# A decoder layer on one core: where the causal mask of the row-maximum pass is added

## The chip, the cores and the metric

The kernel runs on one core of a Trainium2 chip. The metric is device time in microseconds (us): 653.34 us is the median of three runs of the kernel before, which lie between 652.88 and 656.06.

## The reference

A decoder layer with post-norm: causal self-attention, cross-attention to 64 context rows, a mixture of 16 experts of which each token takes 4, and a shared expert, each followed by a layer norm. x is 2 x 1024 x 256 in float32; 16 heads of 16. The change touches the first part alone:

```python
scores = jnp.einsum('bhqd,bhkd->bhqk', Q, K) / math.sqrt(d_k)
causal = jnp.tril(jnp.ones((seq_len, seq_len), dtype=bool))
scores = jnp.where(causal, scores, -jnp.inf)
probs = jax.nn.softmax(scores, axis=-1)
attn = jnp.einsum('bhqk,bhkv->bhqv', probs, V)
```

## The kernel before

**Projection phase** (list `P1`, the first 76 us). Eight tiles of Q or K (`QK`, n = 0 to 7), each 128 x 1024, are projected by TensorE (L1526). So that bf16 products reach float32 accuracy, each tile is cut into three bf16 parts: ScalarE takes the first (L772), VectorE the rest (L978), ScalarE the second (L777), GpSimd the third (L670). SP stores the three parts to DRAM (`qk_parts`, L517). There are two buffers, so ScalarE's tile n waits for the store of tile n - 2 (L770). V is projected in eight further steps (`v`, L1541), the last four behind the last Q/K tile.

**Stacks.** The 32 heads (2 batches x 16) are handled in 8 groups of 4. For a group, `load_stack` (L486) brings 6 combinations of parts of Q and of K from DRAM into `qs` and `ks`, 12 transfers of 128 KB; they fill contraction rows 0 to 95 (`KR`). Three sets of stacks rotate (`g % 3`). Set 0 is loaded behind tile 1's store, set 1 behind tile 4's, set 2 behind the first row maxima, the others behind the B products of the group that used the set. In rows 96 to 98 (`KR` to `KM`) K has ones and Q the negative row maximum in three bf16 parts. The ones are written once, by GpSimd's first instruction, for rows 96 to 127 of all three sets (L657); rows 99 to 127 are never read. VectorE's first instruction waits for that memset and for all the others at GpSimd's start (`filled`, L934).

**A pass (row maxima).** 38 jobs a group (`A_JOBS`): TensorE multiplies a tile of 128 queries with up to 512 keys over 96 rows (L1471), VectorE takes the maximum (L947). Three PSUM banks rotate, so job n waits until VectorE is through with job n - 3 (L1468). Where the last 128 columns lie on the diagonal, a second product per head adds the mask: the identity matrix times `causA`, which has -1e30 above the diagonal (L1476). That is 32 products a group.

**Chain of the maxima ("M").** VectorE joins the maxima and cuts them into three bf16 parts, TensorE transposes them (L1496), ScalarE copies them to `mrow` (L800), SP spreads them with three transfers into rows 96 to 98 of `qs` (L531). The next group's B pass waits for all three (`m_loaded`, L1484).

**B pass.** 24 jobs a group: transposed scores minus the maximum over 99 rows (L1488), exponential on ScalarE (L791), the diagonal's upper part set to zero on GpSimd (L690), the product with V (L1512). `step_order` (L99) writes one order for all engines: each group's B jobs with the A jobs of the next group between them (30 in slots 0 to 16), M at slot 19, and the first 8 A jobs of the group after the next in slots 17 to 23. Before group 0's B jobs come 8 A jobs of group 1.

The queue of SP is in program order: loads, stores, stacks, the three transfers of M, and the row sums. A DMA raises its semaphore by 16 when it has landed.

Of the kernel before, what the change touches and what calls it, by code (L numbers as in the profile page):

```python
# [31 lines left out]
P = 128  # L32
# [17 lines left out]
NEG = -1e30  # L50
MASKED = -4e15
HG = 4
# [7 lines left out]
KM = KR + 3  # L60
CH = 512
# [127 lines left out]
def build(nc, a, out, qk_parts, l_dram, slots, sums_of, marks):  # L189
    with ExitStack() as ctx:  # L190
# [97 lines left out]
        causA = sb("caus_a", [P, P], BF16)  # L288
# [48 lines left out]
        earlier = causA  # L337
# [131 lines left out]
        def _(sp):  # L469
# [13 lines left out]
            for dst, name in ((identb, "identb"), (causA, "causA")):  # L483
                sp.dma_start(dst[:], a[name]).then_inc(ld_caus, 16)

            def load_stack(g, which=(0, 1)):  # L486
                b, o, g2 = g // GB, g % GB // 2, g % 2
                for t in which:
                    dst, split = ((qs, SPLIT_Q), (ks, SPLIT_K))[t]
                    for at, part in enumerate(split):  # L490
                        src = qk_parts[t, b, o, part, 64 * g2:64 * g2 + 64, :].rearrange("(h r) n -> r h n", h=HG)
                        sp.dma_start(dst[at * DH:(at + 1) * DH, g % 3], src).then_inc(ld_stack[g % 3], 16)
# [22 lines left out]
            for n, (b, o, t) in enumerate(QK):  # L515
                sp.wait_ge(part_c, n + 1)
                sp.dma_start(qk_parts[t, b, o].rearrange("s p n -> p s n"),  # L517
                             parts[:, n % 2]).then_inc(stored[n % 2], 16)
                if n == 1:
                    sp.wait_ge(filled, 2)  # L520
                    sp.wait_ge(stored[0], 16)
                    load_stack(0, (0,))
                    sp.wait_ge(stored[1], 16)
                    load_stack(0, (1,))
                if n == 4:
                    load_stack(1)
            for g in range(NG):
                sp.wait_ge(m_row, g + 1)
                for s in range(3):
                    n = HG * TB  # L530
                    sp.dma_start(qs[KR + s:KR + s + 1, g % 3].rearrange("o h s -> o (h s)"),  # L531
                                 mrow[s * n:(s + 1) * n, :]).then_inc(m_loaded, 16)
# [122 lines left out]
        def _(pool):  # L655

            nc.gpsimd.memset(ks[KR:P], 1.0).then_inc(filled, 1)  # L657
            pool.wait_ge(filled, 1)
# [7 lines left out]
            nc.gpsimd.memset(nmx[:], 3e38).then_inc(filled, 1)  # L666
            nc.gpsimd.memset(half[:], -0.5).then_inc(filled, 1)
# [98 lines left out]
        def _(act):  # L766
# [17 lines left out]
            def group(g, order):  # L784
                for kind, n in order:
# [11 lines left out]
                    if kind == "M":  # L797
                        act.wait_ge(m_T, g + 2)
                        wait(act, m_loaded, g * 48 + 48)
# [655 lines left out]
        def _(pe):  # L1455
            def group(g, order):

                u = g % 3
                for kind, n in order:
                    if kind in ("A", "A2"):  # L1460
                        i, c, w, h0, nh = A_JOBS[n]
                        ga = g + (1 if kind == "A" else 2)
                        ua = ga % 3
                        if n == 0:
                            pe.wait_ge(ld_stack[ua], ga // 3 * 192 + 192)
# [3 lines left out]
                        diag = P * (i + 1) <= CH * (c + 1)  # L1469
                        for s in range(nh):  # L1470
                            last = nc.tensor.matmul(ps[:, A_BANKS[n % 3], w * s:w * s + w],  # L1471
                                                    qs[0:KR, ua, h0 + s, P * i:P * i + P],
                                                    ks[0:KR, ua, h0 + s, CH * c:CH * c + w],
                                                    start=True, stop=not diag)
                            if diag:
                                last = nc.tensor.matmul(ps[:, A_BANKS[n % 3], w * (s + 1) - P:w * (s + 1)], identb[:], causA[:],  # L1476
                                                        start=False, stop=True)
                        last.then_inc(a_ready, 1)
                    if kind == "B":
# [3 lines left out]
                        if n == 0:  # L1483
                            pe.wait_ge(m_loaded, g * 48 + 48)  # L1484
# [32 lines left out]
            for kind, n in P1:  # L1517
# [27 lines left out]
                else:  # L1545
                    if kind == "A" and n == 0:
                        pe.wait_ge(ld_caus, 16 * 2)
# [349 lines left out]
```

## Time and profile before

| | us |
|---|---|
| median of 3 runs | 653.34 |
| span of the profiled execution (its own time is not given beside the span) | 708.7 |
| TensorE busy | 612.1 (86%) |
| VectorE busy | 469.8 (66%) |
| ScalarE busy | 351.4 (50%) |
| GpSimd busy | 317.3 (45%) |
| L1471 score products, 384 records | 106.8 |
| L1476 identity products, 256 records | 51.3 |
| L947 row maxima, 304 records | 182.1 |

TensorE's matmuls are pipelined and their ends modelled, so 51.3 us are not 51.3 us of the engine's time: the distance between the starts of two products says what one holds it for. Times in the trace count from the span's start; the projection phase ends at 76, group 0 to 7 lie between 80 and 308, behind them the cross-attention and the experts.

### The profile page before, as it was taken

The page shows a single profiled execution, that of the slowest core. Times are in us where ns is not written, and L with a number is a line of the kernel's source. Part 1 is how long each engine was busy: PE and PEld are TensorE (multiplying, and loading weights), DVE is VectorE, ACT ScalarE, POOL GpSimd, SP SyncE. Part 2 cuts the span into 40 slices and gives each one's busy share as a digit, 9 for nine tenths or more (in the row PEclk, how much of TensorE's full clock was granted, in tenths as well). Part 3 has the DMA queues.
Part 4 walks back from the last instruction along what each step waited for, and adds up shares of the span by engine and source line. Part 5 has one row for each costly group of instructions (what it writes and reads, how often), then busy time and mean ns, then how long its engine had stood idle before and what let it go on. Part 6 is the DMA issues. An engine that isn't in the chain of part 4 may idle for free.

```text
span 708.7 us, 12877 instructions
## 1 busy us (share of the span) xinstructions
PE 612.1 (86%) x3830; PEld 369.6 (52%) x3830; DVE 469.8 (66%) x1303; ACT 351.4 (50%) x734; POOL 317.3 (45%) x393
## 2 busy tenths in 40 slices
PE   6878999999999999898799997959743899889885
PEld 3434434434443343254457765746443788877752
DVE  0369788788787886039658783825442766767687
ACT  1312266666766667734555542423131555556544
POOL 8413313233442432444875336362745455555550
PEclk9989899999999999999999998788985999999999
DMA  5767776146263400009400002120344675548847
GB/s 166 170 169 151 146 226 93 43 68 89 38 93 58 53 19 18 19 16 350 157 1 1 1 27 95 33 97 32 113 141 124 190 207 180 155 147 285 275 173 237
DMA packets 52673, 82.51 MB, mean 116 GB/s; under 512 B 11984, under 2 KB 29648, under 8 KB 52304
## 3 DMA queue, kind: packets, MB, share of 16 engines
q1 hardware_dynamic: 45744, 62.26, 35.7%
q0 software_dynamic: 6864, 19.44, 7.5%
q8 instruction: 34, 0.56, 0.4%
q14 instruction: 31, 0.25, 0.1%
HBM read 53.38 MB, written 32.48 MB: 121 GB/s over the span
## 4 chain that ended last, share of the span: by engine, by line
PE 64%; DVE 15%; issue 5%; another core or an unknown queue 4%; DMA 4%; ACT 4%; POOL 3%; SPq 1%; POOLq 0%; ACTq 0%; DVEq 0%
PE ps L1512 9%; PE ps L1488 9%; PE ps L1777 9%; PE ps L1471 8%; DVE neg_max L947 5%; PE ps L1800 5%; PE ps L1675 4%; PE ps L1694 3%; PE ps L1756 2%; PE ps L1789 2%; PE ps L1684 2%; PE ps L1476 2%; PE ps L1620 2%; PE ps L1711 2%
## 5 line engine op out<-in xcount | busy, mean ns | idle before, releaser
L947 DVE TENSOR_REDUCE neg_max<-ps 128x1 f32<-128x512 f32 (+3 forms) x304 | 182.1, 654 | 45.0 <-PE ps L1476 28.1
L791 ACT ACTIVATE temps<-ps 128x1024 f32<-128x1024 f32 (+1 forms) x192 | 147.6, 812 | 81.5 <-PE ps L1488 81.5
L690 POOL TENSOR_SCALAR_AFFINE_SELECT temps<-temps 128x256 f32<-128x256 f32 x128 | 52.2, 411 | 151.8 <-ACT temps L791 150.8
L1471 PE MATMUL ps<-stacks 96*128 96x512 bf16 (+3 forms) x384 | 106.8, 336 | 11.1 <-DMA stacks<-qk_parts 5.2
L761 POOL DMA_INDIRECT expert_outputs<-x_T,w_o_xqkv x79 | 77.4, 980 | 69.2 <-ACT x_T L911 40.5
L1488 PE MATMUL ps<-stacks 99*128 99x512 bf16 (+3 forms) x384 | 95.3, 334 | 3.3 <-DMA stacks<-m_rows 1.7
L1512 PE MATMUL ps<-temps,v_group 128*32 128x512 f32 (+3 forms) x768 | 82.7, 502 | 1.7 <-ACT temps L791 0.9
L1777 PE MATMUL ps<-w_split,block_x 128*128 x474 | 73.3, 292 | 6.3 <-issue 3.3
L754 POOL DMA_INDIRECT expert_slots<-x_tok,w_o_xqkv x64 | 62.3, 974 | 28.7 <-issue 17.2
L1777 PEld LDWEIGHTS ps<-w_split,block_x 128*128 128x128 f32 x474 | 64.3, 196 | 8.3 <-issue 8.1
L1488 PEld LDWEIGHTS ps<-stacks 99*128 99x128 bf16 x384 | 27.5, 99 | 77.1 <-ACT temps L791 50.9
L1471 PEld LDWEIGHTS ps<-stacks 96*128 96x128 bf16 x384 | 37.7, 99 | 48.7 <-DVE neg_max L947 20.2
L724 POOL TENSOR_TENSOR ln_rstd<-ln_var_eps,minus_half 128x1 f32<-128x1 f32 x32 | 18.8, 588 | 73.5 <-DVE ln_var_eps L1021 73.5
L1476 PE MATMUL ps<-caus_a,ident_b 128*128 128x128 bf16 x256 | 51.3, 226 | 0.0
L1800 PE MATMUL ps<-w_split,block_h 128*128 x237 | 49.5, 318 | 0.2 <-ACT x_T L911 0.2
L1374 DVE TENSOR_TENSOR o_norm<-ps,o_norm 128x128 f32<-128x128 f32 x79 | 22.5, 284 | 35.6 <-ACT o_norm L898 29.8
L1789 PE MATMUL ps<-ident_f,o_norm 128*128 128x128 f32 x79 | 23.8, 301 | 25.7 <-DVE o_norm L1374 19.5
L898 ACT ACTIVATE o_norm<-ps 128x128 f32<-128x128 f32 x79 | 22.3, 283 | 45.8 <-PE ps L1777 27.2
L849 ACT ACTIVATE o_norm<-o_norm 128x512 f32<-128x512 f32 x32 | 20.2, 630 | 48.4 <-DVE o_norm L1268 45.7
L1352 DVE TENSOR_TENSOR block_x<-ps,block_x 128x256 fp32r<-128x256 f32 x79 | 33.0, 419 | 11.6 <-issue 7.1
L890 ACT ACTIVATE block_x<-ps 128x256 fp32r<-128x256 f32 x79 | 31.1, 393 | 14.9 <-PE ps L1756 8.8
L1526 PE MATMUL ps<-x_T,w_qkv 128*128 128x512 f32 x64 | 32.4, 648 | 6.9 <-DMA x_T<-in_xT 6.9
(219 smaller groups left out, 1089.7 us busy)
## 6 DMA issues: line engine op xcount, KB each, us to landing
stacks<-qk_parts SPq DMA_DIRECT2D x96, 128.0 KB, 5.8
v_group<-expert_slots SPq DMA_DIRECT2D x79, 138.5 KB
qk_parts<-temps SPq DMA_DIRECT2D x8, 768.0 KB, 4.4
w_raw<-in_w SPq DMA_DIRECT2D x4, 1024.0 KB, 10.2
early_parts<-expert_outputs SPq DMA_DIRECT2D x4, 1024.0 KB
expert_slots<-in_pad SPq DMA_DIRECT2D x16, 138.5 KB
expert_slots<-in_pad SPq DMA_DIRECT2D x1, 2077.5 KB
x_T<-in_xT SPq DMA_DIRECT2D x4, 512.0 KB, 7.0
```

The costliest lines, as they stand in the source:

```text
L690: nc.gpsimd.affine_select(diag, diag, [[0, 2], [1, P]], ALU.is_ge, zero, base=0, channel_multiplier=-1).then_inc(b_cut, 1)
L754: pool.indirect_dma_start(slots, bass.IndirectOffsetOnAxis(ridx[:, t, k:k + 1].bitcast(U32), 0), xe[:, t, :], None).then_inc(scattered[q], 16)
L761: pool.indirect_dma_start(sums_of, bass.IndirectOffsetOnAxis(idxs[:, b:b + 1].bitcast(U32), 0), yb[:, b % YB, :], None).then_inc(landed[b ...
L791: nc.scalar.activation(pt[:, n % 4, :, 0:w], ps[:, 2 + 2 * (n % 2):4 + 2 * (n % 2), 0:w], ACT.Exp, scale=SCALE).then_inc(b_exp, 1)
L947: nc.vector.tensor_reduce(nmx[:, c, h0:h0 + nh, i], ps[:, A_BANKS[n % 3], 0:w * nh].rearrange("p (h k) -> p h k", h=nh), axis=AX.X, op=ALU ...
L1471: last = nc.tensor.matmul(ps[:, A_BANKS[n % 3], w * s:w * s + w], qs[0:KR, ua, h0 + s, P * i:P * i + P], ks[0:KR, ua, h0 + s, CH * c:CH * ...
L1476: last = nc.tensor.matmul(ps[:, A_BANKS[n % 3], w * (s + 1) - P:w * (s + 1)], identb[:], causA[:], start=False, stop=True)
L1488: last = nc.tensor.matmul(ps[:, bank, 0:w], ks[0:KM, u, 2 * pr + s, P * j:P * j + P], qs[0:KM, u, 2 * pr + s, q0:q0 + w], start=True, stop ...
L1512: last = nc.tensor.matmul(ps[HS * h:HS * h + HS, 6, CH - w:CH], vg[:, u, j, h, :], pt[:, (2 * p + h // 2) % 4, h % 2, 0:w], start=(j == 0) ...
L1777: last = nc.tensor.matmul(ps[:, 2 + b % 2, 0:D], xsp[b % 3][:, xp, k, :], w13s[:, bass.ds(expert[b], 1), wp, at:at + 2 * INTER], start=(k ...
L1789: nc.tensor.transpose(ps[:, 4 + b % 2, 0:P], hblk[:, b % 3, :], identf[:]).then_inc(hb_T, 1)
L1800: last = nc.tensor.matmul(ps[:, 6 + b % 2, 0:D], hsp[:, b % 3, hp, :], w2s[:, bass.ds(expert[b], 1), wp, :], start=(n == 0), stop=(n == 2))
```

## The change

The contraction rows 96 to 127 hold a mask during the A pass. `q_mask` and `k_mask` are matrices of 32 rows whose product is very negative where the key comes after the query within a block of 128, and between 0 and -1 elsewhere, small against what the row maximum is for. The diagonal tile is one product over all 128 rows, and the columns before it are another over 96 rows; the identity products, `causA` and their part of the chain are gone. Where all columns are diagonal there is one product instead of two.

Rows 99 to 127 are loaded once for each of the three sets, by `load_mask_rows` (29 rows of 8 KB, for Q and for K): set 0 ahead of the projection's stores, sets 1 and 2 behind tile 4's store and ahead of `load_stack(1)`. Rows 96 to 98 are loaded by `load_stack` each time (3 rows of 8 KB, for Q and for K), and before the B pass the ones are brought to K by one more transfer (`m_ones`, 24 KB) ahead of the three of M. GpSimd's memset of rows 96 to 127 is gone; the memset of `nmx` is cut in two, which leaves the count of `filled` as it was.

```diff
@@ load, SP @@
-            for dst, name in ((identb, "identb"), (causA, "causA")):
-                sp.dma_start(dst[:], a[name]).then_inc(ld_caus, 16)
+            sp.dma_start(identb[:], a["identb"]).then_inc(ld_caus, 16)
+            mask_rows = (a["q_mask"], a["k_mask"])
+
+            def load_mask_rows(u):
+                for dst, rows in zip((qs, ks), mask_rows):
+                    sp.dma_start(dst[KM:P, u].rearrange("m h s -> m (h s)"), rows[KM - KR:]).then_inc(ld_caus, 16)
+
+            load_mask_rows(0)
...
                     dst, split = ((qs, SPLIT_Q), (ks, SPLIT_K))[t]
+                    sp.dma_start(dst[KR:KM, g % 3].rearrange("m h s -> m (h s)"),
+                                 mask_rows[t][0:KM - KR]).then_inc(ld_stack[g % 3], 16)
...
                 if n == 1:
-                    sp.wait_ge(filled, 2)
                     sp.wait_ge(stored[0], 16)
...
                 if n == 4:
+                    load_mask_rows(1)
+                    load_mask_rows(2)
                     load_stack(1)
             for g in range(NG):
                 sp.wait_ge(m_row, g + 1)
+                sp.dma_start(ks[KR:KM, g % 3].rearrange("o h s -> o (h s)"), a["m_ones"]).then_inc(m_loaded, 16)
@@ GpSimd @@
-            nc.gpsimd.memset(ks[KR:P], 1.0).then_inc(filled, 1)
-            pool.wait_ge(filled, 1)
+            nc.gpsimd.memset(half[:], -0.5).then_inc(filled, 1)
...
-            nc.gpsimd.memset(nmx[:], 3e38).then_inc(filled, 1)
-            nc.gpsimd.memset(half[:], -0.5).then_inc(filled, 1)
+            for c in range(NC):
+                nc.gpsimd.memset(nmx[:, c], 3e38).then_inc(filled, 1)
@@ TensorE @@
+                        if n == 0 and ga == 1:
+                            pe.wait_ge(ld_caus, 16 * 7)
                         if n == 0:
-                            pe.wait_ge(ld_stack[ua], ga // 3 * 192 + 192)
+                            pe.wait_ge(ld_stack[ua], ga // 3 * 224 + 224)
...
+                        plain = w - P if diag else w
                         for s in range(nh):
-                            last = nc.tensor.matmul(ps[:, A_BANKS[n % 3], w * s:w * s + w],
-                                                    qs[0:KR, ua, h0 + s, P * i:P * i + P],
-                                                    ks[0:KR, ua, h0 + s, CH * c:CH * c + w],
-                                                    start=True, stop=not diag)
+                            if plain:
+                                last = nc.tensor.matmul(ps[:, A_BANKS[n % 3], w * s:w * s + plain],
+                                                        qs[0:KR, ua, h0 + s, P * i:P * i + P],
+                                                        ks[0:KR, ua, h0 + s, CH * c:CH * c + plain],
+                                                        start=True, stop=True)
                             if diag:
-                                last = nc.tensor.matmul(ps[:, A_BANKS[n % 3], w * (s + 1) - P:w * (s + 1)], identb[:], causA[:],
-                                                        start=False, stop=True)
+                                last = nc.tensor.matmul(ps[:, A_BANKS[n % 3], w * s + plain:w * s + w],
+                                                        qs[:, ua, h0 + s, P * i:P * i + P],
+                                                        ks[:, ua, h0 + s, CH * c + plain:CH * c + w],
+                                                        start=True, stop=True)
...
-                            pe.wait_ge(m_loaded, g * 48 + 48)
+                            pe.wait_ge(m_loaded, g * 64 + 64)
```

## Rows read from the trace of the kernel before

**Rows 1.** The page: span, and the chain that ended last by line.
```profile
span 708.7 us, 12877 instructions
PE ps L1512 9%; PE ps L1488 9%; PE ps L1777 9%; PE ps L1471 8%; DVE neg_max L947 5%; PE ps L1800 5%; PE ps L1675 4%; PE ps L1694 3%; PE ps L1756 2%; PE ps L1789 2%; PE ps L1684 2%; PE ps L1476 2%; PE ps L1620 2%; PE ps L1711 2%
```

**Rows 2.** Windows: length, busy time (x instructions) by engine, TensorE clock, DMA share, GB/s.
```profile
80.00:86.50 6.50, 6.50 (x32) 2.95 (x34) 4.99 (x9) 3.52 (x4) 1.23 (x3) 0.59 1.08 160
115.35:144.20 28.85, 28.64 (x230) 11.88 (x233) 24.02 (x45) 19.40 (x27) 7.50 (x18) 1.00 0.45 69
```

**Rows 3.** Chain of waits inside one group: start us, us, what.
```profile
119.33 0.06 PE ps L1476
...
121.05 0.22 PE ps L1471
...
140.43 3.09 DVE neg_max L947 x5
```

**Rows 4.** Timeline of the projection phase: start us, us, engine line op, [idle before <-releaser].
```profile
0.80 10.33 POOL L657 MEMSET stacks<- 32x12288 bf16 x1 [0.29 <-POOLq L1881]
...
15.44 1.22 DVE L978 TENSOR_TENSOR temps<-ps,temps 128x1024 f32<-128x1024 f32 x1 [15.44 <-POOL minus_half L667]
...
23.64 1.02 ACT L772 ACTIVATE temps<-ps 128x1024 bf16<-128x1024 f32 x1 [2.62 <-DMA qk_parts<-temps]
...
39.66 1.02 ACT L772 ACTIVATE temps<-ps 128x1024 bf16<-128x1024 f32 x1 [8.59 <-DMA qk_parts<-temps]
...
57.43 15.71 SPq L517 DMA_DIRECT2D qk_parts<-temps  x3
...
66.76 1.02 ACT L772 ACTIVATE temps<-ps 128x1024 bf16<-128x1024 f32 x1 [3.07 <-PE ps L1526]
```

**Rows 5.** Chain of waits in the projection phase.
```profile
29.85 8.07 DMA stacks<-qk_parts
...
38.33 0.11 PE ps L1476
...
45.04 0.07 PE ps L1476
```

**Rows 6.** Groups by line and shape in one group: weight loads, busy us, mean ns.
```profile
L1471 PEld LDWEIGHTS ps<-stacks 96*128 96x128 bf16 x48 | 4.6, 97 | 3.9 <-DVE neg_max L947 1.2
...
L1476 PEld LDWEIGHTS ps<-caus_a,ident_b 128*128 128x128 bf16 x32 | 3.1, 98 | 1.2
```

**Rows 7.** Timeline around the end of the chain of the maxima.
```profile
134.62 0.22 PE L1496 MATMUL ps<-ident_b,m_parts 128*96 128x128 bf16 x1
...
135.85 1.82 SPq L531 DMA_DIRECT2D stacks<-m_rows  x3
...
139.51 0.60 PE L1488 MATMUL ps<-stacks 99*128 99x512 bf16 x2
```

**Rows 8.** DMA issues of the page: count, KB each, median us to landing.
```profile
qk_parts<-temps SPq DMA_DIRECT2D x8, 768.0 KB, 4.4
...
stacks<-m_rows SPq DMA_DIRECT2D x24, 8.0 KB, 1.9
```

**Rows 9.** Chain of waits at the one late landing.
```profile
223.59 3.43 DMA stacks<-m_rows
```

**Rows 10.** DMA in 0 to 15 us: GB/s in 40 slices, packets, share.
```profile
GB/s 0 0 0 0 0 0 82 167 393 369 311 273 180 153 224 246 268 306 246 270 358 344 350 361 380 374 371 388 402 368 350 223 88 22 0 0 0 0 0 0
DMA packets 2192, 2.95 MB, mean 197 GB/s; under 512 B 400, under 2 KB 1168, under 8 KB 2192
...
q1 hardware_dynamic: 2192, 2.95, 61.1%
```

**Rows 11.** DMA in 309.4 to 311.4 us, one transfer of 4 rows (16 KB).
```profile
q1 hardware_dynamic: 8, 0.02, 3.0%
```

**Rows 12.** DMA in 335 to 346 us, large packets: packets, MB, share.
```profile
q1 hardware_dynamic: 1447, 3.38, 80.5%
```

**Rows 13.** DMA in 24 to 40 us: GB/s in 40 slices.
```profile
GB/s 241 379 384 307 241 266 220 384 189 159 154 159 159 118 159 149 169 143 169 108 164 154 159 154 154 154 118 164 154 164 133 200 230 389 410 410 410 405 410 404
```

More of the change, by code:

```diff
@@ L49 @@
 SCALE = DH ** -0.5
-NEG = -1e30
 MASKED = -4e15
@@ L60 @@
 KM = KR + 3
+MROWS = P - KR
+MBLK = P // MROWS
+MSTEP, MTOP, MFAR = 31, 46, 80
 CH = 512
@@ L287, in build @@
         identb = sb("ident_b", [P, P], BF16)
-        causA = sb("caus_a", [P, P], BF16)
+        earlier = sb("earlier", [P, P], BF16)
         identf = sb("ident_f", [P, P], F32)
@@ L336, in build @@
         slot_base = nm[:].rearrange("p u n -> p (u n)")[:, 0:2 * E].bitcast(BF16)
-        earlier = causA
         assert stacks_at == vg_at + 4 * 3072 and temps_at == stacks_at + 4 * 20480
@@ L798, in group @@
                         act.wait_ge(m_T, g + 2)
-                        wait(act, m_loaded, g * 48 + 48)
+                        wait(act, m_loaded, g * 64 + 64)
                         nc.scalar.activation(mrow[:], ps[0:3 * HG * TB, 0, 0:64].bitcast(BF16),
@@ L1546, in _ @@
                     if kind == "A" and n == 0:
-                        pe.wait_ge(ld_caus, 16 * 2)
+                        pe.wait_ge(ld_caus, 16 * 3)
                         pe.wait_ge(v_kept, 4)
@@ L1867 @@
     data["identb"] = (row == col).astype(bf)
-    data["causA"] = np.where(col > row, NEG, 0.0).astype(bf)
+    block, at = np.arange(P) // MBLK, np.arange(P) % MBLK
+    mine = np.arange(MROWS)[:, None] == block[None, :]
+    after = block[None, :] > np.arange(MROWS)[:, None]
+    q_mask = np.where(mine, np.ldexp(1.0, MTOP - MSTEP * at)[None, :], 0.0)
+    k_mask = np.where(mine, -np.ldexp(1.0, MSTEP * at - MTOP)[None, :], np.where(after, -np.ldexp(1.0, MFAR), 0.0))
+    data["q_mask"] = np.tile(q_mask, (1, HG * TB)).astype(bf)
+    data["k_mask"] = np.tile(k_mask, (1, HG * TB)).astype(bf)
+    data["m_ones"] = np.ones((KM - KR, HG * S), bf)
     data["earlier"] = (row < col).astype(bf)
```

## The prediction

> **What bounds the kernel now.** I read the page first, for the order of size [rows 1]: the lines of TensorE lead the chain that ended last, and the identity products (L1476) are 2% of it, so some 14 us is all that taking them out could give. The span is 708.7 us; no other time of the profiled execution is given, and the median of the runs is 653.34 us. All times below are differences in the profiled execution, taken over unscaled to the median; the first 110 us, where most of them lie, may be a few per cent shorter without the profiler. The measurement of this kernel can tell about 0.5% (3.3 us) from no change.
>
> Next the windows. One group takes 28.85 us, with TensorE busy for 28.64 of them and VectorE for 24.0 [rows 2]. Then the chain inside one group: product follows product with no gap; an identity product holds TensorE for 0.06 us, a score product of 512 columns for 0.22, and in one place VectorE binds, 3.09 us for five reductions [rows 3]. Before the groups stands the projection phase (0 to 76 us). There the chain runs over the loads into the stacks and over VectorE: GpSimd's first memset (10.33 us) holds VectorE's first operation to 15.44, ScalarE waits 8.59 us for a store, its last projection tile is taken at 66.76 [rows 4], and the last stack load lands at 37.92 [rows 5]. That phase decides this case.
>
> **The products.** In a diagonal tile the change streams w columns where w + 128 were streamed. A weight load takes 97 ns for 96 rows and 98 for 128 [rows 6], so the taller contraction costs nothing, and it lies beside products as before. One group has 32 identity products, 32 x 0.057 = 1.8 us. Not all of it is won, since TensorE may run only three banks ahead of VectorE. Going through one group in its order: two products stand before the wait for the five reductions and four before the job at which TensorE meets VectorE a second time; these six only lengthen waits. Seven stand behind the transposition of the maxima. The other 19 give 1.1 us between a group's first B product and the transposition.
>
> **The chain of the maxima.** From the transposition (134.62) to the next group's first B product (139.51) are 4.89 us [rows 7]. Inside lie ScalarE's exponential and copy, then three DMA issues from 135.85, 0.61 apart, and the last lands 1.9 us after its issue [rows 8]: 135.85 + 1.22 + 1.87 = 138.94, that is 0.57 us early. The change issues one more DMA ahead of the three (the ones), +0.61, so 139.55; TensorE without its seven products would be there at 139.11. It waits 0.45 us, and this stretch comes to 4.98 us. A group so gives 1.1 - 0.1 = 1.0 us; groups 1 to 5 give 4.9. Where a landing takes 3.43 us, as once [rows 9], TensorE waits in both kernels, and the group gives 0.4 less. In group 6 the DMA ended the stretch already: I take 0.1. Group 0 runs part of its products at half clock (0.59 in 80 to 86.5 [rows 2]), where each is 0.11 us: 1.2 us. In the projection phase VectorE binds; I take 0.9 us, nearly all from the cold products at 38 to 42 and 76 to 80. Sum of the products: **-7.1 us**.
>
> **GpSimd and SP.** The 10.33 us memset is gone. What remains ahead of VectorE is some 4.5 us long, so its first operation is held only by ScalarE, at 13.3 (-2.1). The stack loads get one more issue each side (0.43 us): -1.6 at the first score product if nothing else changed. In the groups the two 24 KB mask transfers are issued behind the maxima and needed more than 20 us later, at nothing: SP idles there, and without that cover they would cost 0.9 us a group. The 24 KB of ones goes out ahead of three transfers that end later; nothing beyond its issue.
>
> **The mask rows.** Six new transfers of 29 rows of 8 KB (238 KB each) go to the queue of SP: two behind the first nine loads, four between store 4 and the loads of stack 1. What they cost hangs on how many of the 16 DMA engines carry one, and no row has a transfer of 29 rows. What rows have: the first nine transfers, all of 128 rows, leave 400 packets under 512 B [rows 10], which are the 256 rows of the two small matrices and 9 x 16 = 144 completion packets, sixteen each. The one transfer of 4 rows leaves 8 packets, 4 of data and 4 of completion [rows 11]: four engines, one row each. So the rows go out in equal shares. 29 is prime and more than 16, so it has no equal shares over several engines. **I take one engine.** The Trainium skill ("DMA: Bandwidth & Descriptors", section "Why a DMA increments its semaphore by 16 and not by 1") says just this of a count not shown here: the number of engines is the largest up to 16 that divides the slowest dimension of both sides, and 127 partitions get one. By its rule 29 rows get one engine too; by its bandwidth table (27 GiB/s an engine) one transfer would take 8.2 us.
>
> The price of one: large packets moved 3.38 MB in 0.805 x 16 x 11 us, 23.9 KB per engine-us [rows 12], so 238 KB take **10 us**. The best slices have 410 GB/s over 16 engines, 25.6 [rows 13]: 9.3 us. The first loads have 2.95 MB in 0.611 x 16 x 15 us, 20.1 [rows 10]: 11.8 us. The far ends are 0.7 us (spread over sixteen, two rows each) and 24 us (155 GB/s over 16, the rate of the stack loads [rows 13]). I take 10, since long rows are nearest to the long packets.
>
> That engine serves what is queued in order, as the wait for store 2 shows: it was queued behind the stack loads, which land at 37.92, and ScalarE had it only at 39.66 [rows 4, 5], where the median store lands in 4.4 us [rows 8]. So:
> - Start. The first loads end at 12.4 (the 33rd of 40 slices of 15 us [rows 10]). The two mask transfers hold the engine to 32.4. Store 0 has 1/16 of its 768 KB on it (2 us) and lands at 35, not 23.6. ScalarE's third tile and the first stack load wait for it. The stack loads (1.57 MB at 155 GB/s, 10 us, the second half issued from 38) land at 46.2, not 37.9: the first score product is 8 us late, and the tile that waits for store 2 (39.66) as well. In general 2p - 12 for a price p.
> - Middle. Store 4, as late as the products, goes out at 55, the engine is free at 57.4, then four mask transfers to 97.4, its share of the stack 1 loads to 101.5, of store 5 to 103.5. ScalarE's last projection tile waits for store 5 to leave its buffer: 104, not 66.76. VectorE's part of it, 1.6 us behind ScalarE's start before and 1.1 now, starts at 105.1, not 68.3, and behind it stand the chain of the first maxima, the last three V projections, the stores 6 and 7 and group 0. The shift is 36.8 us, in general 6p - 23.2. The memset's 2.1 us are hidden by this wait.
> - TensorE idles some 25 us there and comes back at 1.2 GHz. After the pause before 38.06 its identity products took 0.11 us, and 0.07 from 45 on [rows 5]; of the time at half rate I take 1.9 us as new, in the V projections.
>
> Sum: +36.8 + 1.9 - 7.1 = +31.6, and 653.3 + 31.6 = **685 us**.
>
> **The rivals.** (a) The 29 rows are spread over fifteen or sixteen engines, about 1 us each. Then nothing waits for them: at the start the queue idles from 12.4 to 20, in the middle SP is done with its issues at 56, before store 5 (57.4). The products' 7.1 us and the 1.6 us of the start come out: 644.6 us. Against it: the equal shares of [rows 10, 11]. It decides as soon as a transfer takes under about 4 us (6p = 23). (b) One engine, and at the rate of the stack loads, p = 24.5: shift 124 us, 772 us. Against it: those loads write 16 partitions from sixteen engines at once, these use one. (c) Spread, but the fourth DMA in the chain of the maxima makes every landing as late as the one of 3.43 us [rows 9]: the stretch becomes 1.23 + 1.83 + 3.43 + 0.05 = 6.5 us, each group loses 1.65 - 1.1 = 0.6, seven of them 4, against 3.7 won before them (1.6, 0.9 and 1.2): 653.6 us, no change. Against it: the median of the 24 landings is 1.9 us [rows 8]. (d) The change doesn't do what it says: would the mask rows not mask, the row maximum would only be larger and no time would change; it has no case of its own.
>
> **The numbers.** One engine at 8 to 13 us: 0.82. (a) 0.12, (b) 0.03, (c) 0.03. From them faster 0.12, same 0.03, slower 0.85. The range takes p from 7.9 to 12.8, which covers the bounds 9.3 and 11.8 and a projection phase that may be shorter unprofiled: 672 to 702.
>
> **What would show it.** In the changed profile: ScalarE waits for a store at 23 to 35 and, for some 30 us, before its last projection tile; windows in which the DMA share stays near 1/16 and 24 GB/s; group 0's first B product at about 118 us, not 80; a group of 27.9 us with a wait of about 0.4 us for the m_rows transfer; no 10 us memset. It is wrong if the mask transfers land within some 3 us; if they take one engine at another rate, the size is off by 6 us for each us of p; if a group stays at 28.85 us, the fourth DMA took the gain back.

## The result: slower by 40 us, and the profile after

| us | before | after |
|---|---|---|
| median (4 runs each) | 653.16 | 693.33 |
| lowest to highest | 652.88 to 656.06 | 688.63 to 695.01 |
| ratio to before, 95% interval | | 1.0594 (1.0551 to 1.0636) |
| span of the profiled execution | 708.7 | 691.1 |

The change makes the kernel 6% slower, and the forecast was 685 (672 to 702). Medians and ranges here are of all runs; the ratios leave out the few slow ones (more than 1.5% above their kernel's fastest, one each of e1_even and e9_moved below). Each ratio below is to runs of the kernel before taken beside that experiment (medians 652.9 to 653.8). The two spans stand the other way round. Group 7's first B product, before and after:

```profile
284.02 1.04 PE L1488 MATMUL ps<-stacks 99*128 99x512 bf16 x4 [0.74 <-DMA stacks<-m_rows]
...
321.02 1.08 PE L1504 MATMUL ps<-stacks 99*128 99x512 bf16 x4 [1.32 <-DMA stacks<-m_rows]
```

Behind it, where nothing was changed, lie 424.7 us before and 370.1 after. In the profiled executions of all other kernels below, that part is 369 to 378 us long too, so the one of before was stretched there, in nothing that the change touches; everything below is read in the first 321 us. Up to group 7 the trace shows +37.0 us and the medians +40.2. The 3.2 us between them lie with the profiled execution of before as well: a kernel's own time is some 2 us above its span, and 284.0 + 370.1 + 2.0 would be 656.1, the longest of its runs and 3 us over their median.

The page of the kernel after: span, busy time by engine, the chain that ended last by engine and by line, and one row of the DMA issues (count, KB, median us to landing).

```profile
span 691.1 us, 12778 instructions
...
PE 590.6 (85%) x3766; PEld 360.5 (52%) x3766; DVE 472.3 (68%) x1303; ACT 354.7 (51%) x734; POOL 307.5 (44%) x393
...
PE 45%; DVE 19%; DMA 12%; SPq 9%; issue 5%; POOL 5%; ACT 4%; POOLq 0%; DVEq 0%; ACTq 0%
PE ps L1504 8%; PE ps L1528 7%; DVE neg_max L957 6%; PE ps L1793 5%; DMA qk_parts<-temps 4%; PE ps L1485 4%; SPq L501 4%; POOL expert_slots L764 3%; PE ps L1816 3%; PE ps L1691 2%; PE ps L1710 2%; DMA v_group<-expert_slots 2%; DMA stacks<-m_rows 2%; SPq L497 2%; PE ps L1636 2%
...
qk_parts<-temps SPq DMA_DIRECT2D x8, 768.0 KB, 10.4
```

Against [rows 1], the identity products are out of the chain, and DMA (12%) and SP's own issuing (SPq, 9%) are in it. The median store of three parts took 4.4 us [rows 8] and takes 10.4. So the place to look is the transfers, not the compute engines.

ScalarE in the projection phase of the kernel after (start us, us, engine line op, idle before and its releaser); the first row answers to the tile at 23.64 in [rows 4], the second to 39.66, the third to 66.76:

```profile
32.74 1.02 ACT L782 ACTIVATE temps<-ps 128x1024 bf16<-128x1024 f32 x1 [13.05 <-DMA qk_parts<-temps]
...
47.95 1.02 ACT L782 ACTIVATE temps<-ps 128x1024 bf16<-128x1024 f32 x1 [8.58 <-DMA qk_parts<-temps]
...
109.06 1.02 ACT L782 ACTIVATE temps<-ps 128x1024 bf16<-128x1024 f32 x1 [37.92 <-DMA qk_parts<-temps]
```

ScalarE waits three times for a store, for 59.6 us in sum. The last tile carries the whole result: 109.06 against 66.76 is 42.3 us, more than the 40.2 between the medians.

What the DMA engines did meanwhile, in 14 to 32 us of the kernel after (GB/s in 40 slices of 0.45 us, then the queue's packets, MB and share of 16 engines), and in 59 to 71 us (slices of 0.3 us):

```profile
GB/s 18 36 18 18 36 18 36 18 36 18 36 18 314 378 410 378 296 27 18 150 400 396 391 396 68 36 18 36 18 18 36 18 36 18 36 18 23 23 27 27
...
q1 hardware_dynamic: 826, 1.95, 27.9%
...
GB/s 27 27 27 27 27 27 27 27 27 27 27 27 27 27 27 27 27 27 27 27 27 27 27 27 27 27 27 27 27 27 27 27 27 27 27 27 27 27 27 27
...
q1 hardware_dynamic: 41, 0.33, 6.5%
```

One packet of 8 KB in 0.45 us is 18 GB/s, two are 36. Outside the two bursts, the first of them beginning within 1 us of SP's issue of store 0 (18.57), packets of 8 KB pass one behind another. In 59 to 71 us they are alone: one row in each 0.306 us, 26.8 GB/s, at 1/16 of the engines' time (6.5%). The 29 rows of one transfer so take 8.9 us, and the 58 of set 0 pass from 12.45 to 30.3 us. The bursts are the shares of store 0 and store 1 on the other fifteen. Each is moved within 3 us, and the part on the one engine stands behind the mask rows.

SP's queue in the kernel after (start us, us spent on issuing, line, transfer):

```profile
55.58 1.30 SPq L489 DMA_DIRECT2D stacks<-in_q_mask  x1
56.92 5.66 SPq L489 DMA_DIRECT2D stacks<-in_k_mask  x1
62.62 9.46 SPq L497 DMA_DIRECT2D stacks<-in_q_mask  x1
72.12 10.39 SPq L501 DMA_DIRECT2D stacks<-qk_parts  x6
82.56 2.97 SPq L497 DMA_DIRECT2D stacks<-in_k_mask  x1
85.57 10.19 SPq L501 DMA_DIRECT2D stacks<-qk_parts  x6
95.81 19.21 SPq L526 DMA_DIRECT2D qk_parts<-temps  x3
```

The forecast had nothing of this. An issue that costs 0.3 to 0.45 us elsewhere takes 9.46 here, near the 8.9 of one mask transfer, and six stack loads take 10.39 where they took 2.68 at 32.98. SP itself is held, so store 5 is not issued at 57, to stand in a queue, but at 95.81, and lands 13.2 us later. What it waits for in these 13.2 us, the DMA view of 98 to 109 us shows (GB/s in 40 slices of 0.275 us):

```profile
GB/s 0 30 30 30 30 149 387 387 417 365 387 380 335 425 410 372 425 372 395 380 179 22 52 0 30 22 22 30 22 22 22 30 22 30 22 22 30 22 30 22
```

The burst from 99.4 us on is stores 5 and 6 on the other engines, and from 103.8 on only one engine works. By the packets' sizes the last mask row leaves it at 102.0, the shares of the stack 1 loads follow to 106.6, and store 5's share, 24 packets of 2 KB, passes from 106.6 to 108.5. So store 5 would have stood behind the mask rows of this engine wherever SP had issued it after them.

Two windows of the V projections after the pause (length; busy time of PE, PEld, DVE, ACT, POOL; granted clock; DMA share; GB/s), then the same work before, then one whole group from B product to B product:

```profile
111.48:115.10 3.62, 3.62 (x9) 2.77 (x10) 1.40 (x6) 0.95 (x1) 2.12 (x1) 0.50 0.00 0
115.10:119.77 4.67, 4.67 (x18) 3.65 (x16) 1.51 (x4) 0.27 (x1) 1.38 (x1) 0.79 0.52 186
...
69.60:71.40 1.80, 1.79 (x8) 1.53 (x9) 1.40 (x6) 0.95 (x1) 0.77 (x1) 1.00 0.00 0
71.40:75.20 3.80, 3.73 (x18) 2.96 (x16) 1.54 (x5) 0.27 (x1) 1.36 (x1) 1.00 0.40 153
...
237.31:265.07 27.76, 27.18 (x217) 10.95 (x218) 24.22 (x45) 19.19 (x27) 9.75 (x18) 1.00 0.44 73
```

TensorE had been idle for 35.2 us and comes back at a granted clock of 0.50, the lower level. The V projections take 8.3 us, where before the same work ran at clock 1.00 in 5.5. The group is 27.76 us against 28.85 [rows 2]. The chain of the maxima in one group of the kernel after, beside [rows 7]:

```profile
176.30 0.22 PE L1512 MATMUL ps<-ident_b,m_parts 128*96 128x128 bf16 x1
...
177.63 0.26 SPq L539 DMA_DIRECT2D stacks<-in_m_ones  x1
...
177.93 1.82 SPq L542 DMA_DIRECT2D stacks<-m_rows  x3
...
181.07 0.60 PE L1504 MATMUL ps<-stacks 99*128 99x512 bf16 x2 [0.19 <-DMA stacks<-m_rows]
```

The added transfer delays the three others by 0.30 us, and TensorE waits 0.19 us for the last. From group 0's first B product to group 7's are 196.66 us, against 203.95 before: -7.3.

### The profile page after: what moved, and what is told of

Its sections match the earlier page's. It is cut to its first block, busy times and chain, and to the rows that moved or that the text cites. A ratio compares the mean times of both kernels' runs of the same rounds, so it can differ in the third digit from the quotient of the medians.

```text
span 691.1 us, 12778 instructions
## 1 busy us (share of the span) xinstructions
PE 590.6 (85%) x3766; PEld 360.5 (52%) x3766; DVE 472.3 (68%) x1303; ACT 354.7 (51%) x734; POOL 307.5 (44%) x393
## 3 DMA queue, kind: packets, MB, share of 16 engines
q1 hardware_dynamic: 45924, 64.24, 36.1%
## 4 chain that ended last, share of the span: by engine, by line
PE 45%; DVE 19%; DMA 12%; SPq 9%; issue 5%; POOL 5%; ACT 4%; POOLq 0%; DVEq 0%; ACTq 0%
PE ps L1504 8%; PE ps L1528 7%; DVE neg_max L957 6%; PE ps L1793 5%; DMA qk_parts<-temps 4%; PE ps L1485 4%; SPq L501 4%; POOL expert_slots L764 3%; PE ps L1816 3%; PE ps L1691 2%; PE ps L1710 2%; DMA v_group<-expert_slots 2%; DMA stacks<-m_rows 2%; SPq L497 2%; PE ps L1636 2%
## 5 line engine op out<-in xcount | busy, mean ns | idle before, releaser
L771 POOL DMA_INDIRECT expert_outputs<-x_T,w_o_xqkv x79 | 78.0, 988 | 34.9 <-issue 17.7
L1485 PE MATMUL ps<-stacks 96*128 96x512 bf16 (+3 forms) x320 | 87.0, 320 | 7.1 <-DVE neg_max L957 6.7
L680 POOL TENSOR_TENSOR temps<-temps 128x1024 bf16<-128x1024 f32 x8 | 17.0, 2124 | 89.7 <-ACT temps L787 89.7
L1557 PE MATMUL ps<-w_qkv,x_T 128*128 128x256 f32 x64 | 19.6, 466 | 42.7 <-DVE temps L988 35.2
L988 DVE TENSOR_TENSOR temps<-ps,temps 128x1024 f32<-128x1024 f32 x8 | 9.8, 1219 | 66.6 <-ACT temps L782 66.6
L1485 PEld LDWEIGHTS ps<-stacks 96*128 96x128 bf16 x320 | 30.9, 98 | 39.1 <-DVE neg_max L957 21.4
L1490 PE MATMUL ps<-stacks 128*128 128x128 bf16 x256 | 44.4, 221 | 4.6 <-DMA stacks<-qk_parts 1.9
L782 ACT ACTIVATE temps<-ps 128x1024 bf16<-128x1024 f32 x8 | 8.2, 1021 | 77.7 <-DMA qk_parts<-temps 59.6
L1542 PE MATMUL ps<-x_T,w_qkv 128*128 128x512 f32 x64 | 34.4, 681 | 7.1 <-DMA x_T<-in_xT 7.1
L1557 PEld LDWEIGHTS ps<-w_qkv,x_T 128*128 128x128 f32 x64 | 14.8, 238 | 47.5 <-issue 45.1
## 6 DMA issues: line engine op xcount, KB each, us to landing
qk_parts<-temps SPq DMA_DIRECT2D x8, 768.0 KB, 10.4
```

What stands on the lines that cost most here:

```text
L771: pool.indirect_dma_start(sums_of, bass.IndirectOffsetOnAxis(idxs[:, b:b + 1].bitcast(U32), 0), yb[:, b % YB, :], None).then_inc(landed[b ...
L1490: last = nc.tensor.matmul(ps[:, A_BANKS[n % 3], w * s + plain:w * s + w], qs[:, ua, h0 + s, P * i:P * i + P], ks[:, ua, h0 + s, CH * c + p ...
L1557: last = nc.tensor.matmul(ps[:, V_BANKS[n], D * i:D * i + D], xT[:, k, P * (2 * n + i):P * (2 * n + i) + P], wqkv[:, k, 2 * D:3 * D], star ...
```

## The experiments

My theory, which the first four test: a transfer of 29 rows stays on one engine, costs about 10 us there, and all behind it waits; the products themselves are a gain of 7. The rival: the mask data (1.4 MB) or its place in SP's order costs the time, however it is divided.

**e1_even.** The 29 rows go as 16 + 13 rows, in the same places; data and order stay.

```diff
+MASK_PARTS = (((3, 19, 0, 4), (19, 32, 0, 4)), ...
-                    sp.dma_start(dst[KM:P, u].rearrange("m h s -> m (h s)"), rows[KM - KR:]).then_inc(ld_caus, 16)
+                    for r0, r1, h0, h1 in MASK_PARTS[u]:
+                        sp.dma_start(dst[KR + r0:KR + r1, u, h0:h1].rearrange("m h s -> m (h s)"),
+                                     rows[r0:r1, S * h0:S * h1]).then_inc(ld_caus, 16)
```

> The changed kernel, but each mask transfer of 29 rows is cut into two, of 16 and of 13 rows: same bytes, same places in the queue, twelve issues instead of six. Theory (a transfer goes in equal shares, 29 rows on one engine, 16 on sixteen and 13 on thirteen): each takes about 1 us or less, ScalarE's wait for a store before its last projection tile is gone, and the time is 644 us (653.3 less 7.1 for the products, less 1.6 for GpSimd's memset), 641 to 648. Rival (the cost is the 1.4 MB of mask data, or the place of the transfers ahead of the stores): still 685 to 695 us.

Measured: 657.36 us (10 runs, 655.29 to 665.35), ratio 1.0061 (1.0024 to 1.0098). The division of the same bytes over other engines takes 36.0 us out of 693.3. But it stays 13 us over the expected time. Where, the chain of waits (start us, us, what) and ScalarE's last tile of e1_even show, and the DMA view of 46 to 75 us:

```profile
57.20 15.47 DMA qk_parts<-temps
```
```profile
72.75 1.02 ACT L789 ACTIVATE temps<-ps 128x1024 bf16<-128x1024 f32 x1 [9.29 <-DMA qk_parts<-temps]
```
```profile
GB/s 0 105 381 282 249 407 102 136 150 62 138 161 155 79 138 110 122 136 138 133 124 133 141 136 138 127 150 184 175 201 198 172 189 325 328 339 316 198 57 0
...
q1 hardware_dynamic: 2404, 4.93, 92.5%
```

Store 5 is issued at 57.20, on time, and takes 15.47 us. The engines are busy for 92.5% and move some 135 GB/s for half the window, the rate of the stack loads [rows 13], not the 350 to 410 of the stores. From 51 to 57 us, where most packets are mask rows, the mean is 128 GB/s. So spread mask rows cost here what stack loads cost; both write few partitions (13 or 16), but that this is the reason was not tried. 0.95 MB at 135 to 155 GB/s is 6 to 7 us more ahead of store 5. ScalarE has its last tile 6.0 us later than before (72.75 against 66.76), after a wait of 9.29; in the changed kernel it was 42.3.

**e2_half, e3_start, e4_middle.** The same program with other divisions: half of each row (two of four heads) as 29 rows and half as 16 + 13; 29 rows for set 0 alone; 29 rows for sets 1 and 2 alone.

```diff
 e2_half
+MASK_PARTS = (((3, 32, 0, 2), (3, 19, 2, 4), (19, 32, 2, 4)), ...   # all three sets
 e3_start
+MASK_PARTS = (((3, 32, 0, 4),), ((3, 19, 0, 4), (19, 32, 0, 4)), ((3, 19, 0, 4), (19, 32, 0, 4)))
 e4_middle
+MASK_PARTS = (((3, 19, 0, 4), (19, 32, 0, 4)), ((3, 32, 0, 4),), ((3, 32, 0, 4),))
```

> The changed kernel, but only half of each mask row goes as 29 rows (4 KB each, one engine); the other half goes as 16 and 13 rows. Same bytes. Theory: the price p of one single-engine transfer is halved to some 5.1 us; by 6p - 23.2 the shift against the kernel before is 7 us less the gains of 7.1 and part of the 1.6: 650 to 658 us, so far less than half of the loss is left. Rival (loss in proportion to bytes, or to the number of issues): 690 us or more.

> The changed kernel, with the 29-row form only for the first set of stacks (two transfers at the start); sets 1 and 2 go as 16 and 13 rows. Theory: the first score product comes at 46.2 as in the changed kernel (8.2 us later than before), the middle costs nothing: 653.3 + 8.2 - 7.1 = 654 us, 651 to 658. Rival (the start is hidden, all of the loss is in the middle): 645 us.

> The changed kernel, with the 29-row form only for sets 1 and 2 (four transfers in the middle); set 0 goes as 16 and 13 rows. Theory: the start is 1.6 us earlier than before, so the middle's chain starts some 10 us earlier than in the changed kernel and its wait stays as long: 693.3 - 10 = 683 us, 679 to 687. Rival (the end of the middle is set by something that does not move with the start): 693 us.

| | us (n) | ratio, 95% | over e1_even |
|---|---|---|---|
| e1_even | 657.36 (10) | 1.0061 (1.0024 to 1.0098) | |
| e2_half | 669.74 (4) | 1.0225 (1.0156 to 1.0295) | +12.4 |
| e3_start | 664.35 (4) | 1.0143 (1.0075 to 1.0211) | +7.0 |
| e4_middle | 686.25 (4) | 1.0473 (1.0392 to 1.0555) | +28.9 |
| the change | 693.33 (4) | 1.0594 (1.0551 to 1.0636) | +36.0 |

Start and middle add up: 7.0 + 28.9 = 35.9. Their waits for a store, e3_start first, then e4_middle:

```profile
33.33 1.02 ACT L789 ACTIVATE temps<-ps 128x1024 bf16<-128x1024 f32 x1 [12.90 <-DMA qk_parts<-temps]
...
82.19 1.02 ACT L789 ACTIVATE temps<-ps 128x1024 bf16<-128x1024 f32 x1 [9.52 <-DMA qk_parts<-temps]
```
```profile
22.92 1.02 ACT L789 ACTIVATE temps<-ps 128x1024 bf16<-128x1024 f32 x1 [2.55 <-DMA qk_parts<-temps]
...
101.57 1.02 ACT L789 ACTIVATE temps<-ps 128x1024 bf16<-128x1024 f32 x1 [37.21 <-DMA qk_parts<-temps]
```

e3_start has the change's wait at the start (12.90 against 13.05) and e1_even's at the end (9.52 against 9.29); e4_middle has it the other way round (37.21 against 37.92). Each wait follows its own transfers. The waits carry the times: 37.21 less e1_even's 9.29 is 27.9 of e4_middle's 28.9. The expected 650 to 658 and 654 of e2_half and e3_start were too low by 12 us and 10 us, about what e1_even itself was over; in e4_middle (3 us over) the long wait covers the term of e1_even. Half the bytes on one engine cost 12.4 us, a third of 36, and ScalarE's waits for a store sum to 36.1 us there, to 22.0 in e1_even and 59.6 in the change. Bytes and place in the order are the same in all five kernels, so the rival falls as the reason of the 36 us; of the data and its place remain the 6 us of e1_even's last tile.

**e5_act_queue.** If an engine serves its queues side by side, the order in SP's queue is what hurts, and the mask rows could stay in 29 rows on a queue of their own. All six go out from ScalarE's queue: set 0 behind its tile 0, set 1 behind tile 3, set 2 behind tile 7, each with its own semaphore.

```diff
+            def load_mask_rows(u):
+                for dst, rows in zip((qs, ks), mask_rows):
+                    for r0, r1, h0, h1 in MASK_PARTS[u]:
+                        nc.scalar.dma_start(dst[KR + r0:KR + r1, u, h0:h1].rearrange("m h s -> m (h s)"),
+                                     rows[r0:r1, S * h0:S * h1]).then_inc(ld_mask[u], 16)
...
+                if n == 0:
+                    load_mask_rows(0)
...
+                if n == 3:
+                    load_mask_rows(1)
...
+            load_mask_rows(2)
```

> The changed kernel with the same six transfers of 29 rows, but issued from ScalarE's queue instead of SP's: set 0 behind its first tile, set 1 behind its fourth, set 2 behind its last; each set is waited for by its own first product. Same engine, same bytes, another queue. Theory (a store is late because its share stands behind the mask rows in the same queue of the engine): the stores pass, ScalarE's wait before the last projection tile falls from 38 us to under 10, 650 to 662 us. Rival (the engine itself is taken, whatever the queue): 680 us or more.

Measured: 687.04 us (5 runs, 684.7 to 692.67), ratio 1.0499 (1.0416 to 1.0581); the trace is of the slowest of the five. The long wait ahead of the last tile is gone, as the theory said, but the time is the rival's. Two pieces of its chain of waits, ScalarE's wait at the start, a row of SP's queue, and the two queues in 26 to 32 us (packets, MB, share; q10 is ScalarE's, q1 SP's):

```profile
22.12 17.70 DMA qk_parts<-temps
...
42.83 17.27 DMA qk_parts<-temps
```
```profile
31.70 1.02 ACT L790 ACTIVATE temps<-ps 128x1024 bf16<-128x1024 f32 x1 [11.81 <-DMA qk_parts<-temps]
```
```profile
102.29 27.33 SPq L552 DMA_DIRECT2D w_o_xqkv<-in_wo  x1
```
```profile
q10 hardware_dynamic: 15, 0.12, 4.8%
q1 hardware_dynamic: 16, 0.03, 1.3%
```

Store 0, which has no transfer before it in SP's queue but the first loads, lands 12.8 us after its issue; store 1, behind it, takes 17.70, and store 2, behind the stack loads, 17.27. The last two lines say why: while both queues have work, the engine passes one row of 8 KB and one packet of 2 KB in turn, a row each 0.386 us where it was 0.306. A store neither passes the rows nor waits for all of them; each of its 24 packets on this engine waits for one row. ScalarE still waits 11.81 us at the start, then 4.83, 16.90 and 6.76, and group 0's first B product starts at 98.08 (e1_even 87.09, the change 124.36). The loss then comes in group 0, which takes 45.27 us where the change's takes 28.91: set 2's mask rows are awaited for 8.5 us, and SP stands for 27.33 us at one issue of the late loads (5.01 before), ahead of the chain of the maxima. So the queue is not the resource; the engine is. That SP is held by the engine too is how I read that row; no run here separates it.

**e8_no_identity.** What the identity products are worth by themselves: the kernel before without them and with nothing in their place, so that the row maximum is taken over later keys too.

```diff
-                                                    start=True, stop=not diag)
-                            if diag:
-                                last = nc.tensor.matmul(ps[:, A_BANKS[n % 3], w * (s + 1) - P:w * (s + 1)], identb[:], causA[:],
-                                                        start=False, stop=True)
+                                                    start=True, stop=True)
```

> The kernel before without the identity products and with nothing in their place: the row maximum is then taken over the keys after the query too; no other line changes, no DMA is added. It measures the products' term alone. Theory: a group goes from 28.85 to 27.4 us (19 products before the transposition, 7 behind it, 0.057 each, no fourth DMA), the whole to 653.8 - 10 = 644 us, 641 to 647. Rival (VectorE binds as soon as TensorE is relieved, so that the groups keep their length): 651 us or more.

Measured: 645.14 us (4 runs, 643.2 to 648.12), ratio 0.989 (0.9806 to 0.9973). One group of e8_no_identity:

```profile
130.33:157.83 27.50, 27.06 (x195) 9.71 (x193) 24.23 (x45) 19.19 (x28) 9.75 (x18) 1.00 0.43 69
```

27.50 against 28.85 is 1.35 us for 32 products, of the 1.8 that they hold TensorE for. This is the most that another place for the mask could give in a group. The time lies where it was expected (644, 641 to 647), and with the shorter groups the rival falls.

**e9_moved and e7_kept_ones.** Two versions that keep the gain. e9_moved has 16 + 13 rows and issues set 1 behind store 3 and set 2 behind the loads of stack 2, where the queue has room. e7_kept_ones does the same with another mask: blocks of 5 instead of 4 columns a row need 26 rows (99 to 124), so rows 96 to 98 hold K's ones beside them, and 125 to 127 are zero. All 32 rows then are one transfer, and neither K's three rows in each stack load nor the fourth transfer in the chain of the maxima is needed.

```diff
 both
-                if n == 4:
+                if n == 3:
                     load_mask_rows(1)
-                    load_mask_rows(2)
+                if n == 4:
                     load_stack(1)
...
                     load_stack(2)
+                    load_mask_rows(2)
 e7_kept_ones
+MBLK = 5
+MROWS = -(-P // MBLK)
-                    sp.dma_start(dst[KM:P, u].rearrange("m h s -> m (h s)"), rows[KM - KR:]).then_inc(ld_caus, 16)
+                    sp.dma_start(dst[KR:P, u].rearrange("m h s -> m (h s)"), rows).then_inc(ld_caus, 16)
-                sp.dma_start(ks[KR:KM, g % 3].rearrange("o h s -> o (h s)"), a["m_ones"]).then_inc(m_loaded, 16)
```

> The even cut (16 and 13 rows) with two sets moved in the queue: set 1 behind tile 3's store, set 2 behind the loads of stack 2; everything else as in the even cut, the ones in the chain of the maxima too. Theory: the 6.4 us by which store 5 was late come from the mask data that stood between store 4 and the loads of stack 1, so they vanish, and with them the V projections at half clock: 657.4 - 8 = 649 us, 645 to 652. Rival (store 5 is late for another reason, or the data costs as much elsewhere): 656 us.

> The better version that the runs point to. The mask takes 26 rows (blocks of 5 columns) instead of 32, so rows 96 to 98 keep K's ones for good and only Q's three rows are set to zero again for each reuse of a set; the transfer of ones leaves the chain of the maxima. All 32 rows go in one transfer (sixteen engines), set 0 at the start, set 1 behind tile 3's store where the queue idles, set 2 behind the loads of stack 2. Theory: the wait before the last projection tile is gone (-9 against the even cut), a group takes 27.5 us instead of 27.8 (-2): 657.4 - 11 = 646 us, 641 to 649, faster than both kernels. Rival (the mask data costs its 6 us wherever it stands in the queue): 654 us.

Measured: e9_moved 652.24 us (10 runs, 646.45 to 657.07), ratio 0.9967 (0.9924 to 1.0009); e7_kept_ones 647.73 us (10 runs, 644.65 to 651.76), ratio 0.9917 (0.9880 to 0.9954). e9_moved can't be told from the kernel before and lies just above its expected range (645 to 652): its last tile is on time (66.50), but in its trace three of the waits for `m_rows` are long (1.77, 0.67 and 1.32 us). e7_kept_ones is faster than the kernel before (by 0.8%) and than the change, as expected (641 to 649). ScalarE's last tile (not held by a store any more), group 0's first B product, and a group of e7_kept_ones:

```profile
63.80 1.02 ACT L784 ACTIVATE temps<-ps 128x1024 bf16<-128x1024 f32 x1 [2.96 <-PE ps L1544]
```
```profile
76.70 1.06 PE L1506 MATMUL ps<-stacks 99*128 99x512 bf16 x2
```
```profile
129.19:156.73 27.54, 27.12 (x220) 10.96 (x217) 24.24 (x45) 19.20 (x28) 9.76 (x18) 1.00 0.46 74
```

Group 0's first B product is at 76.70 (before 80.07, e9_moved 79.41), and the group at 27.54 is within 0.05 us of e8_no_identity's: the taller contraction costs nothing that can be seen. Between transpositions e9_moved's groups take 27.78. The difference, 0.24 us a group, goes with the fourth transfer: it lies between transposition and B product (4.76 against 4.51 us), and TensorE's waits for `m_rows` agree (3.2 us in six up to group 6 in e9_moved, 0.6 in one in e7_kept_ones).

**e6_memset_last.** The forecast called GpSimd's memset (10.33 us) a gain of 1.6 at the first product. Here the kernel before does it last instead of first.

```diff
-            nc.gpsimd.memset(ks[KR:P], 1.0).then_inc(filled, 1)
-            pool.wait_ge(filled, 1)
...
+            pool.wait_ge(filled, 6)
+            nc.gpsimd.memset(ks[KR:P], 1.0).then_inc(filled, 1)
+            pool.wait_ge(filled, 7)
@@ VectorE @@
-            dve.wait_ge(filled, 7)
+            dve.wait_ge(filled, 6)
```

> The kernel before, with GpSimd's memset of the keys' stacks put behind the memsets that the first normalisation waits for. My theory: VectorE's first operation follows the memsets, so it starts about 2 us earlier (15.44 us to some 13.3), and since the store of the first tile, its stack loads and the first product follow in a chain without slack, the first product and then the whole kernel come some 1.6 us earlier: 651.8 us. Rival: the start waits for the loads of the inputs, whose landing is the same, so VectorE's first operation stays within 0.3 us and the time stays at 653.3 us.

Measured: 651.71 us (6 runs, 649.83 to 659.18), ratio 1.0005 (0.9958 to 1.0052). VectorE's first operation, then the first score product and group 0's first B product of e6_memset_last:

```profile
13.64 1.23 DVE L979 TENSOR_TENSOR temps<-ps,temps 128x1024 f32<-128x1024 f32 x1 [13.64 <-ACT temps L773]
```
```profile
36.31 0.22 PE L1472 MATMUL ps<-stacks 96*128 96x128 bf16 x1 [3.20 <-DMA stacks<-qk_parts]
...
77.37 0.60 PE L1489 MATMUL ps<-stacks 99*128 99x512 bf16 x2
```

In the trace the chain does what was expected: VectorE 1.8 us earlier, the first product too (36.31 against 38.06), the first B product 2.7 (77.37 against 80.07). The time doesn't decide: 1.6 us is 0.25%, inside the interval. Shown is the way of the 1.8 us to the first product, not that the kernel is faster.

## Why the prediction was right

| step | forecast | measured |
|---|---|---|
| engines that carry a 29-row transfer | one | one |
| its price p | 10 us | 8.9 where the rows pass alone (29 x 0.306); 10.9 on average for the four in the middle |
| ScalarE's third tile | 35 | 32.74 |
| first score product | 46.2 | 46.19 |
| ScalarE's last tile | 104 | 109.06 |
| V projections, new cold time | +1.9 | +2.8 |
| group 0's first B product | 118 | 124.36 |
| transposition to B product | 4.98 | 4.77 |
| group | 27.87 | 27.76 to 27.81, once 28.47 |
| products, from group 0's first B product to group 7's | -6.2 | -7.3 |
| total against before | +31.6 | +40.2 |

**One engine** was the step that decided, and it held. In the trace the queue moves 27 GB/s, one row at a time, for as long as mask rows are alone on it, and the stores' bursts pass beside it on the other engines; e1_even takes 36.0 us out by the division alone. The Trainium skill ("DMA: Bandwidth & Descriptors", section "Why a DMA increments its semaphore by 16 and not by 1") gives the number of engines as the largest up to 16 that divides the slowest dimension; the rows of 29 and of 4, and the 16 + 13 that undo the loss, agree with it. Equal shares in [rows 10, 11], and 29 being prime, had given the same.

**The start** came out as forecast, by two errors that cancel. Store 0 landed at 32.7, not 35, because the two mask transfers took 17.9 us, not 20: the price p is 8.9 here, under the lower bound of 9.3 that I took from the best slices. The stack loads then needed 13.4 us from their first issue (32.67 to 46.06), not 11.

**The middle** is where the total was missed. The step "store 4 goes out at 55, ... its share of store 5 to 103.5" had the order on the engine right and one size wrong. From 58.3 to 108.5 us the engine is never idle, and it passes what the forecast listed, in that order: the 116 mask rows to 102.0, the shares of the stack 1 loads and of store 5 to 108.5. The rows begin 0.9 us later than forecast and take 43.7 us, not 40; the two shares take 6.5, not 6.1. That is the 5 us (109.06 against 104). A mask row takes 0.31 us alone and up to 0.95 us at times between 73 and 98 us, when SP's stack loads pass on the other engines; the forecast had no term for that. Over all six transfers the price of 10 us fits (61.6 us for 60), but by luck: it is too high at the start, where rows pass alone, and too low here. The forecast also had nothing of SP being held for 38.9 us (56.92 to 95.81). In this trace that doesn't set the last tile, since store 5's share has to stand behind the rows in any case; what the holding costs by itself no run separates.

**The cold products** were under-sized. I took 1.9 us for the V projections; the first of the three took 3.62 us at clock 0.50 where it had taken 1.8, and the other two 4.67 at 0.79 against 3.7. In e1_even, where TensorE had been idle for 6.6 us and not for 35.2, the first part is as slow (3.62 at 0.50) and the second at full clock (3.70). The late tile (5.1) and the clock (0.9) account for 6.0 of the 6.4 us by which group 0's first B product misses its forecast. The groups give back 1.1, so group 7's starts 5.4 us later than forecast (321.0 against 284.0 + 31.6). The total is off by 8.3; the other 2.9 are the 3.2 us of the first section, a forecast of differences laid on an execution of before that was longer than its median. Whether the profiler or that run made it so stays open.

**The products** were slightly under-sized: group 0 gave 1.7 us (30.60 to 28.91) and not 1.2, groups 1 to 5 gave 5.7 and not 4.9. The fourth transfer costs 0.30 us of delay, where I had taken 0.61 from the spacing of the others, so five of the seven waits before a B pass are 0.16 to 0.20 us, not 0.45. The other two are 0.86 (the group of 28.47) and 1.32, late landings such as one was before [rows 9]; that the mask transfers of the stack loads have no part in them was not tried. In the groups on pace these 24 KB transfers show up nowhere, as forecast. GpSimd's 2.1 us at VectorE (14.02 instead of 15.44 in this trace, 1.4) were hidden, as forecast: the third tile waits for the mask rows on the other side.

**Rival (a)** had its time wrong even for a spread transfer. It said "nothing waits for them"; e1_even is that case, and it takes 657.4 us, not 644.6. What the rival left out is that the spread rows move no faster than the stack loads there and stand ahead of store 5. Moved to where the queue has room they cost little (e9_moved, 652.2), and with the fourth transfer gone as well the time comes to about 3 us from the forecast of 644.6 (e7_kept_ones). Rival (c)'s fourth DMA exists at 0.24 us a group, a seventh of its price. Rival (b)'s rate is excluded by the 27 GB/s.

## What to carry to other kernels

Look at how the row count of every large transfer divides before placing it: here 29 rows, a prime, went to one engine, and the same rows as 16 + 13, or a mask padded to 32 rows, move in a fraction of the time. A slow transfer is paid by what is issued behind it, on that engine whatever the queue, and here by the issuing engine too; look for the store or load that a compute engine waits for next. And a small gain in each of eight groups (here 1 us of 28.85) is worth having only if the setup that it needs is put where its queue is idle.

## What the runs showed of the hardware that was not expected

- **An issuing engine is held.** SP spent 9.46 us on one issue of 24 KB and 10.39 us on six of 128 KB, against 0.30 and 2.68 at other times, while one engine worked off mask rows. What exactly it is held by isn't shown. With half the bytes there (e2_half) the longest six-load stretch was 6.30 us.
- **A second queue gives no second engine.** In e5_act_queue, three stores of 768 KB took 12.8, 17.7 and 17.3 us with the mask rows on the other queue, against 4.4 [rows 8]. The engine served the two queues one packet each in turn.
- **One packet at a time.** Alone, an engine passes a row of 8 KB each 0.306 us (26.8 GB/s). With stack loads on the other engines a row took up to 0.95 us.
- **Spread rows can be slow too.** In e1_even, 16 + 13 rows of 8 KB and stack loads moved at 110 to 141 GB/s for half of a window in which the engines were busy for 92.5%, and stores reach 400.
- **Issues have no one price.** The 24 KB of ones takes 0.26 us to issue and delays what follows by 0.30, where the three transfers behind it are 0.61 apart.
- **After 35.2 us without products** TensorE ran 3.6 us at a granted clock of 0.50 and the next 4.7 at 0.79; after 6.6 us without (e1_even), the first 3.6 us were at 0.50 as well and the next 3.7 at 1.00.
